# A soft mixture-of-experts layer: a slot's maxima over 64 experts by folding the logits in halves, in place of one strided pass over 2048 columns

## The reference

```python
logits = (jnp.einsum('tzd,ed->tze', x, phi_w) + phi_b).reshape(t, z, n, p)   # n = 64 experts, p = 32 slots
D = jax.nn.softmax(logits, axis=3)        # over the 32 slots of an expert
C = jax.nn.softmax(logits, axis=2)        # over the 64 experts of a slot
X_tilde = jnp.einsum('tznp,tzd->npd', D, x)
...
Y = jnp.einsum('tznp,npH->tzH', C, Y_tilde)
```

## Time and profile before

| | |
|---|---|
| time, median of 3 runs | 3861.61 us (3860.94 to 3884.2) |
| the profiled execution's own time | 3860.01 us |
| its span | 3858.2 us |
| busy share of the span | PE 91%, DVE 79%, ACT 58%, POOL 37% |
| mean granted TensorE clock | 0.946 of full |

### The profile page before, as it was taken

How to read it: one execution, slowest core, us unless ns; L and a number is a source line. 1 busy time by engine, 2 the same in 40 slices (tenths; PEclk the granted TensorE clock), 3 DMA queues, 4 the chain that set the end, 5 groups by cost and what they waited for, 6 DMA issues and landing times.

```text
span 3858.2 us, 93855 instructions
## 1 busy us (share of the span) xinstructions
PE 3529.1 (91%) x32894; PEld 2469.3 (64%) x32894; DVE 3049.2 (79%) x11272; ACT 2231.2 (58%) x6991; POOL 1442.1 (37%) x1741
## 2 busy tenths in 40 slices
PE   7999999999999989899989969989878999899855
PEld 6888888888888866666644433335555666555542
DVE  7888888888988866677779967767886778888771
ACT  5888888898888842267654434433333222477611
POOL 2555555545555510145448845520000000222117
PEclk9999999999999989889989989999988999899958
DMA  3000000000000012210000000000000000000023
GB/s 130 3 3 3 3 3 3 3 3 3 3 3 3 3 59 87 62 67 2 2 0 1 0 11 0 1 1 1 1 1 34 1 1 1 34 2 2 23 61 49
DMA packets 30897, 64.58 MB, mean 17 GB/s; under 512 B 3424, under 2 KB 19808, under 8 KB 29152
## 3 DMA queue, kind: packets, MB, share of 16 engines
q1 hardware_dynamic: 24288, 52.29, 3.9%
q0 software_dynamic: 6144, 6.30, 1.0%
HBM read 49.93 MB, written 8.65 MB: 15 GB/s over the span
## 4 chain that ended last, share of the span: by engine, by line
PE 69%; DVE 17%; ACT 5%; issue 5%; POOL 2%; DMA 1%; DVEq 0%; POOLq 0%; ACTq 0%; SPq 0%
PE ps L176 9%; PE ps L536 8%; PE ps L496 7%; PE ps L473 6%; PE ps L520 6%; PE ps L1679 3%; PE ps L1650 3%; PE ps L1648 3%; PE ps L2303 3%; PE ps L2290 2%; DVE gbbc L2342 2%; PE ps L1019 2%; DVE gbbc L2331 2%; DVE gbbc L2337 2%; PE ps L983 2%
## 5 line engine op out<-in xcount | busy, mean ns | idle before, releaser
L741 ACT ACTIVATE T<-T 128x128 f32<-128x128 f32 x1024 | 396.9, 397 | 8.9 <-DVE T L662 8.9
L741 ACT ACTIVATE W<-T 128x128 f32<-128x128 f32 x1024 | 397.2, 399 | 1.3 <-DVE T L662 1.3
L642 DVE CUSTOM_DVE_ANT_0 T<-ps,C 128x128 f32<-128x128 f32 x1536 | 381.3, 286 | 0.0
L652 DVE COPY_PREDICATED W<-gbbc,ps 128x512 f32<-128x512 int32 x512 | 342.7, 722 | 3.2 <-PE ps L176 2.6
L536 PE MATMUL ps<-W,gbbc 64*64 64x128 f32 (+1 forms) x6912 | 316.4, 311 | 2.1 <-DVE W L652 1.2
L496 PE MATMUL ps<-T 64*64 64x192 f32 (+2 forms) x8192 | 313.3, 290 | 4.2 <-DVE T L642 4.1
L176 PE MATMUL ps<-C,T 128*128 128x128 f32 (+1 forms) x1620 | 262.1, 298 | 49.8 <-DVE T L307 18.9
L496 PEld LDWEIGHTS ps<-T 64*64 64x64 f32 x8192 | 254.5, 133 | 77.9 <-issue 45.5
L1246 POOL TENSOR_TENSOR QK<-T,QK 128x512 fp32r<-128x512 f32 x128 | 161.9, 1274 | 376.2 <-ACT T L1206 258.1
L536 PEld LDWEIGHTS ps<-W,gbbc 64*64 64x64 f32 x6912 | 280.2, 133 | 24.9 <-PE ps L536 19.3
L832 POOL TENSOR_TENSOR W<-W,T 128x512 f32<-128x512 f32 x256 | 260.8, 1040 | 78.1 <-DVE T L669 78.1
(11 more groups left out here) (420 smaller groups left out, 8782.9 us busy)
## 6 DMA issues: line engine op xcount, KB each, us to landing
T<-crow_dram SPq DMA_DIRECT2D x128, 128.0 KB, 3.0
W<-in_l1f_dram SPq DMA_DIRECT2D x1, 6152.0 KB, 18.2
W<-in_l0a_dram SPq DMA_DIRECT2D x1, 5172.5 KB, 25.6
W<-in_l2f_dram SPq DMA_DIRECT2D x1, 3160.0 KB, 10.5
W<-in_l3f_dram SPq DMA_DIRECT2D x1, 3076.0 KB, 10.0
W<-in_sm_dram SPq DMA_DIRECT2D x1, 2729.0 KB, 9.2
W<-in_l0f_dram SPq DMA_DIRECT2D x1, 2256.0 KB, 30.4
X<-in_x_dram SPq DMA_DIRECT2D x1, 2048.0 KB, 7.4
```

The lines of the kernel that those rows point to most:

```text
L642: done(e.tensor_tensor_reduce(sm[:, at:at + 128], src, m, 1.0, -3.0e38, ALU.add, ALU.max, mx[:, col:col + 1]), s["masked"], x == (3 if ban ...
L652: e.copy_predicated(a.PT[t % 2][:, 512 + 512 * j:1024 + 512 * j].rearrange("p (h w) -> p h w", h=4), is_.unsqueeze(1).broadcast_to([P, 4, ...
L741: done(e.activation(a.Pr[i % 4][:, at:at + w_], a.Sm[i % 2][:, at:at + w_], ACT.Exp, bias=a.ngs[i % 4][:, c:c + 1], scale=a.scale, accum_o ...
```

## The change

VectorE's one pass L2342 becomes four instructions. The first takes the maximum of the two halves of `f.L` (1024 columns each) into a new buffer `f.fold` and signals `slot`; the second and third halve that again, to 512 and to 256 columns (`f.part`); the fourth is a strided maximum over `f.part`'s 8 groups of 32 and writes `f.mxn`. The fourth is done one round later. The pieces are put between the instructions that were there, so that each waits for a result that another instruction separates it from. `f.small` moves from `gbbc` to `T` to make room for `f.fold`.

```diff
@@ soft_plan
-    f.mxn = rg.get(1024)
+    f.mxn, f.fold = rg.many(2, 1024)
     f.yt = r.get(2048)
-    f.small = rg.many(6, 64)
+    f.small = r.many(6, 64)
...
+    f.part = r.get(256)
@@ soft_dve
+    folded = summed = 0
     for i in range(NT + 1):
         if i < NT:
             e.wait_ge(*s["taken"](4 * i + 4))
...
                             ALU.max).then_inc(s["max"].sem, 1)
         if i >= 1:
             d = i - 1
+            e.wait_ge(c_.sem, folded)
+            c_.then(e.tensor_reduce(f.mxn[:, 32 * d:32 * d + 32], f.part.rearrange("p (n q) -> p q n", q=32), AX, ALU.max))
+        if i < NT:
+            e.tensor_tensor(f.fold, f.L[i % 2][:, 0:1024], f.L[i % 2][:, 1024:2048], ALU.max).then_inc(s["slot"].sem, 1)
+        if i >= 1:
             e.wait_ge(*s["exps"](d + 1))
             past(e, s["inv"], d - 1)
-            c_.then(e.tensor_reduce(f.small[2 + d % 2], f.E[d % 4].rearrange("p (n q) -> p n q", q=32), AX, ALU.add))
-            c_.hold(e)
+            summed = c_.then(e.tensor_reduce(f.small[2 + d % 2], f.E[d % 4].rearrange("p (n q) -> p n q", q=32), AX, ALU.add))
+        if i < NT:
+            e.wait_ge(*s["slot"](i + 1))
+            folded = c_.then(e.tensor_tensor(f.fold[:, 0:512], f.fold[:, 0:512], f.fold[:, 512:1024], ALU.max))
+        if i >= 1:
+            e.wait_ge(c_.sem, summed)
             past(e, s["soft"], d - 1)
             e.reciprocal(f.small[4 + d % 2], f.small[2 + d % 2]).then_inc(s["inv"].sem, 1)
         if i < NT:
-            e.tensor_reduce(f.mxn[:, 32 * i:32 * i + 32], f.L[i % 2].rearrange("p (n q) -> p q n", q=32), AX,
-                            ALU.max).then_inc(s["slot"].sem, 1)
+            e.wait_ge(c_.sem, folded)
+            folded = c_.then(e.tensor_tensor(f.part, f.fold[:, 0:256], f.fold[:, 256:512], ALU.max))
```

## The result

The changed kernel takes 3896.78 us (median of 13 runs, 3883.83 to 3914.98) against 3861.61 (median of 13 runs, 3856.11 to 3888.09). The ratio is 1.009, with a 95% interval of 1.0074 to 1.0106, that is +29 to +41 us. The forecast was 3892, +30.4, "within 1%".

What follows compares the result with a forecast made beforehand. VectorE bounds the loop at 8.59 us a round, TensorE close behind; +24.9 (29 rounds), +3.9 (first two) and +1.6 (end) make +30.4 on 3861.6, so 3892 us; range 3842 to 3905, likeliest 3882 to 3905.

Steps and rivals of the forecast that it cites:

- TensorE's floor: Loop round: TensorE's own minimum, 1.14 + 3.4 + 3.63 = 8.2 us, some 0.4 us below VectorE's 8.59.
- the rival: Loop: folds do not meet GpSimd; 29 rounds give -12, up to 6 more elsewhere; 3843 to 3850 us, chance 0.10.
- The work alone: VectorE's loop instructions without GpSimd: 2.91 us of work replaces 3.70; by starts 7.44 us a round against 8.59.
- The meeting: Loop: folds with two SBUF inputs and GpSimd's instructions block each other; a waiting fold begins 0.14 us before GpSimd's end.
- late hand-over: Loop: a blocked instruction begins at the other's end or later; 9.74 us a round, +40, 3901 us; chance 0.10.
- GpSimd goes first: End of L2487: next L2481 passes the waiting fold L2340; 11.8 us a round, +100, 3962 us; chance 0.10.
- no meeting: Loop: folds run at bare durations beside GpSimd, round falls by 0.4 us; 3843 to 3850 us, chance 0.10.
- The round: Loop from third round on: 4.87 + 4.58 = 9.45 us, 0.86 longer than 8.59; 29 rounds give +24.9.
- the last 0.29 of it: L2481 to L2487: L2487 begins 0.29 us after L2354's start, 0.13 before L2354 ends.
- The first two rounds: Loop start: everything in series, 7.9 and 10.5 us, together 18.4 against 14.5 before, +3.9.
- The end: Loop end, from last expert maxima to end of last multiply: 16.7 us against 15.1 before, +1.6.
- the clock: Loop rounds: TensorE idles about 1.25 us each; occasional stretches at 1.2 GHz eat its slack first, 0 to +3 us.

Runs made afterwards that it cites:

- one_input: Against the changed kernel: the three folds become reduces reading one half each, slot maxima partly left out; 3857.26 us in one execution, round 8.19 us.
- folds_together: Against the changed kernel: same seven instructions, the three folds directly one after another behind the expert maxima, strided maximum last; 3997.57 us, round 12.09 us.
- fold_once: Against the kernel before: one 1024-column fold directly behind the expert maxima, strided maximum over 1024 columns; 3854.63 us against 3869.08, ratio 0.9962.

## Why the prediction was right

- **What bounds the kernel.** VectorE did, with TensorE's floor 0.4 us below: one_input shows the floor at 8.19 us, 8.2 forecast. Its pieces were each 0.1 off and made up for one another: in one_input's timeline L2246 to L2252 is 3.54 where 3.4 was taken, and L2252 to L2244 3.53 where 3.63 was. The whole gain of one_input, 16.8 us, is what the change could have brought at most; the rival gave 12 to 18.
- **The work alone.** Right in all pieces: 1.22 us for 1024 columns (1.21 forecast), 0.68 for 512, 0.58 for the strided 256 (0.59). Only the last fold is off, 0.35 where 0.42 was taken; in folds_together, directly behind the fold that it waits for, it does take 0.43. Why it is shorter elsewhere stays open.
- **The meeting.** Right in kind, in both directions and in the order of turns. A fold that waits gets in between two instructions of GpSimd, 0.12 to 0.14 us before the record of the first one ends, at an end of 3.64 us as at one of 1.27. The rivals "late hand-over" and "GpSimd goes first" did not occur, and "no meeting" was what one_input had to be made for. What the Trainium skill's page "SBUF — State Buffer" says in "Who interferes with whom", that the second to come fully blocks, holds in these rounds, but for these 0.12 to 0.14 us; by the whole time its 3901 us are as near to 3897 as 3892 is, and only the round tells them apart, 9.74 by the page against the measured 9.37. The prediction let only the folds begin at the other's end, though. Had GpSimd's two waited for the end of a fold as well, in place of starting 0.13 ahead of it, the round would have been 3.64 + 0.61 + 0.47 + 0.42 and 3.64 + 1.21, 9.99 us, and the time some 3909 (an estimate from these rows): the page's rule to the letter is farther off than the prediction made it.
- **The round.** 9.45 forecast, 9.37 measured. Counted from where GpSimd's instructions do their own work, L2487 to L2481 took 4.58, as forecast, and L2481 to L2487 4.78 in place of 4.87. The term that is off is the last 0.29 of it, from the start of L2354 until GpSimd may go: the shorter L2354 makes 0.21 of it (2062.63 to 2062.79, and 0.05 in which L2487 stands still).
- **The sum.** The first two rounds, 18.4 forecast, took 18.38. The 29 others brought 29 × 0.77 = +22.4 in place of +24.9. The end, +1.6 forecast, brought +4.1: the last multiply ends 16.7 us after the last L2333, as forecast, but then TensorE has fallen to 1.2 GHz in its gaps and the last gather is 2.5 us late. The forecast looked for the clock in the rounds and gave it 0 to +3 us there; it read 0.64 from 1981.0 to 1995.1, where the rounds were no longer than forecast all the same, and 1.00 from 1995.2 to 2261.3, so it cost nothing in the rounds, and the loss came behind them. Two misses of 2.5 us and opposite sign made the loop's +30.6 meet the forecast's +30.4: that they agree to 0.2 is luck, that they agree to some 3 is not.
- **The whole.** +35.2 between the medians, with +29 to +41 by the ratio, takes in the loop's +30.6; what the other stages add is not settled and within what they differ by themselves.

## What to carry to other kernels

Before replacing a slow pass by several quick ones, look at what they read: an instruction of VectorE with two inputs in SBUF and one of GpSimd that reads SBUF excluded each other here for their full length, so a saving on VectorE turns into a loss when GpSimd is nearly full. Look for such pairs in the trace, as durations far above the least of their kind beside a busy GpSimd; price a round as GpSimd's work plus each fold's and whatever GpSimd waits for behind it, and put the few that pay where GpSimd is idle anyway. And ask first what the second-slowest engine allows: here it was 0.4 us a round, which one fold in place of three already reached.

## What the runs showed of the hardware

- The hold lasts for the whole of a 3.64 us instruction, it is not let go in between: L2338 of folds_together stood still from 2112.84 until 2116.16, 0.14 before the end of L2478 at 2116.30. A reduce pass of the same width and place is not touched (1.21 us, one_input), nor a TENSOR_TENSOR with one input in PSUM (0.67 to 0.69 us, L2383 in the trace before). But not every instruction with a single tensor from SBUF is free: in the trace before L359, a TENSOR_SCALAR of four columns with a median of 0.17 us, takes 1.27 beside L1246, so the reduces of this case say nothing of other operations:

```profile
1654.71 1.26 POOL L1246 TENSOR_TENSOR QK<-T,QK 128x512 fp32r<-128x512 f32 x1
1654.73 1.27 DVE L359 TENSOR_SCALAR rs<-rs 128x4 f32<-128x4 f32 x1
```

- The turn went to whoever had asked first: VectorE's waiting fold ahead of GpSimd's next instruction in all 30 rounds of the changed kernel from the third on, and GpSimd's waiting one ahead of a VectorE fold that came 0.03 us after the end of the one before, in the rounds of folds_together (its second fold takes 4.01 us in all 32). It is no rule without exception: in the earlier trace rows L3009, asked for at 2859.26 while L2932 ran, was passed by L2934 and L2936, which came later but started before the one ahead of them had ended.
- A wait of VectorE for its own result cost nothing with another instruction in between (the seven of one_input ran in 7.34 to 7.36 us a round); between two folds it cost 3.3 us a round in folds_together, not for its own length, 0.03, but for the turn that it gave away.
- A strided maximum of 32 values costs 0.58, 1.04, 1.90 and 3.70 us over 256 (changed kernel; 0.49 in folds_together), 512 (L1393), 1024 (fold_once) and 2048 columns (before), 1.7 to 1.8 ns for each further column. The maxima over neighbouring columns take 2.26 us for 2048 (L2331), 1.1 ns a column.
